# Pacing the first layer's gathers by their own landings instead of by TensorE's marks

## The chip, the cores and the metric

The kernel runs on one core of one Trainium2 chip. The metric is the device time of one execution in microseconds; lower is better. The engines are named as the profile names them: PE is TensorE (PEld its weight loads), DVE is VectorE, ACT is ScalarE, POOL is GpSimd, SP is SyncE. SP, ACT and POOL issue DMAs; POOL alone issues the indirect ones that gather rows by a list of indices.

## The reference

Four graph layers follow each other over 8192 nodes of 32 features and 262144 edges. The edges are sorted by their destination `dst`.

```python
edge_index = jnp.stack([src, dst])
x = _layernorm(x + _L0_gnn_ref(x, L0_gnn_weight, src, dst, edge_type_64), axis=-1)
x = _layernorm(x + _L1_gnn_ref(x, edge_index, edge_weight), axis=-1)
x = _layernorm(x + _L2_gnn_ref(x, edge_index), axis=-1)
x = _layernorm(x + _L3_gnn_ref(x, edge_index, edge_attr_4, edge_attr_32, L3_gnn_W1, ...), axis=-1)
```

The first layer takes for each edge a 32 x 32 matrix by the edge's type, multiplies the source node's row by it and sums the results by destination:

```python
w_e = jnp.take(weight, etypes, axis=0)
h_src = jnp.take(feat, src, axis=0)
msg = jnp.einsum('ei,eio->eo', h_src, w_e)
out = jax.ops.segment_sum(msg, dst, num_segments=N_NODES)
```

The second and third sum source rows by destination, weighted by `edge_weight` and plain. The fourth runs a small network on each edge's 32 attributes and combines its output with the source row.

## The kernel before

**The table and the first layer.** PE multiplies every node's row by all 64 matrices beforehand, and the products are stored in `rel_table` in device memory, 8192 x 64 rows of 32 numbers. The first layer then only gathers one row of this table for each edge and sums by destination. The edges are cut into 128 chunks of 2048: 16 tiles (`TILES`) of 128 edges. One indirect DMA of POOL gathers one tile (128 rows of 128 bytes) into `gathered`, so a chunk is 16 gathers, and the whole first layer 2048. `gather_chunk` issues the 16 gathers of one chunk. It first waits for the chunk's indices (`idx_in[s]`, a load of `key_i` by SP as soon as DVE has released the slot `s`), and each gather raises `rows_in[0][s]` by 16 when it has landed. PE sums the chunk with 16 matmuls against a one-hot matrix (`scatter_chunk`, L1074), which waits for `rows_in`, and DVE adds the sum to `acc` (L1669) and releases the slot.

**The strip rounds.** Beside the first layer the kernel prepares the second and third: it builds for each of 128 strips of destinations a dense matrix of edge weights (`adj`, 2 MB a strip) and one of edge counts (`counts`, 0.5 MB). DVE makes the one-hots (L1637 to L1640), PE multiplies them (L1124, `strip_half`), ACT copies the products out of PSUM (L805, L806) and stores them (`strip_rows`, issues at L808 and L810). Its two staging buffers make ACT wait, before a strip, for the landing of the store of two strips earlier. There are 32 rounds; a round is 4 strips (8 halves, each of 4 groups of 8 matmuls; a matmul of this shape leaves two records in the trace) and, on PE, 3 chunks' scatters, before the halves 0, 3 and 6. So 96 chunks (`EARLY`) are gathered and summed in the rounds, in three slots (`TRIO`). From round 12 on (`AHEAD`) each round also loads two 1 MB pieces of `adj` and multiplies them (L1149).

**The late chunks.** The remaining 32 chunks are summed after the rounds, in four slots, each followed by a set of the second layer's matmuls (L1182).

**POOL's pace.** The semaphore `pe_mark` counts marks. `MARKS_0` names, for each half of a round, the matmuls of `strip_half` that raise it: twelve a round. Before every fourth gather of a round, `marks_0` makes POOL wait for the next mark; `LEAD_0` sets how far POOL is ahead (6 marks, 24 gathers). The wait for the n-th group of four is for mark n - 5 counted in the same way. In the late chunks PE raises two marks a chunk (in the scatter or the set behind it), and POOL waits before every eighth gather, again six marks ahead. The first three chunks are gathered without any pace. The last layer, which gathers from `x_rows` in four slots, already waits every eight gathers for the landing of the gathers before (`RESTS_3`, `rests_3`).

The code here runs if the edges have a regular spread (`is_regular`); another path, untouched, stands behind the test.

## Time and profile before

| | us |
|---|---|
| median of 3 runs | 7251.59 |
| lowest, highest | 7243.55, 7280.37 |
| the profiled execution | 7251.99 |
| its span, first to last instruction | 7250.2 |
| strip rounds, from the second on | 383 to about 3010 |
| late chunks and second layer's matmuls | about 3010 to 3910 |
| third layer | about 3910 to 4220 |
| last layer | 4220 to 7250 |

All the views are of one profiled execution. Times in them are microseconds from the span's start. In the timeline the bracket at the end of a row is how long the engine sat idle before it, and what ended that: another engine's instruction, a DMA's landing, or "issue", which is time in which the engine waited for nothing that the profile shows. "remote" stands for a semaphore's raise for which the profile has no instruction; where records of matmuls are missing, a wait for PE reads so.

### The profile page before, as it was taken

To read this page: it belongs to the slowest core of one execution; us is meant where nothing else is said; L and a number is where in the kernel's file an instruction comes from. 1 tells how busy PE (TensorE), PEld (TensorE's weight loads), DVE (VectorE), ACT (ScalarE), POOL (GpSimd) and SP (SyncE) were. 2 spreads that over 40 slices of the span, in tenths; PEclk is the share of its full clock that TensorE was granted. 3 is DMA by queue.
4 is the path that set the end of the run, shared out by engine and by line. 5 is a ranking of instruction groups with operands and counts; after the bars stand their busy time and mean duration, and the time that the engine had idled before them with its cause. 6 is when DMAs were issued, how large, how long until landed. Compare 5 with 4: busy or idle time off the path is not lost.

```text
span 7250.2 us, 118009 instructions
## 1 busy us (share of the span) xinstructions
PE 5598.4 (77%) x38929; PEld 4300.2 (59%) x38930; DVE 4279.9 (59%) x8297; ACT 2999.4 (41%) x7294; POOL 3945.7 (54%) x4168
## 2 busy tenths in 40 slices
PE   7377777777777777666667668888888888888888
PEld 3177777676776766533333346666666666666666
DVE  4166656655556565311111058877887887888788
ACT  4244444444444444200000045555555555555556
POOL 1445555555555555555550146666666666666665
PEclk7587777777777778666667767777777777777777
DMA  9433333444444444687879601111111111111111
GB/s 318 145 150 145 141 136 130 165 162 149 171 151 163 150 162 163 211 283 269 277 242 296 199 15 25 24 23 24 24 24 23 24 24 23 24 24 24 23 25 24
DMA packets 596643, 865.44 MB, mean 119 GB/s; under 512 B 170833, under 2 KB 418706, under 8 KB 579474
## 3 DMA queue, kind: packets, MB, share of 16 engines
q1 hardware_dynamic: 363858, 385.79, 16.8%
q10 hardware_dynamic: 99520, 406.06, 14.2%
q0 software_dynamic: 133120, 71.57, 5.3%
q8 instruction: 102, 1.67, 0.1%
q14 instruction: 43, 0.35, 0.0%
HBM read 455.19 MB, written 406.85 MB: 119 GB/s over the span
## 4 chain that ended last, share of the span: by engine, by line
PE 37%; issue 24%; POOL 23%; another core or an unknown queue 5%; ACT 5%; DMA 3%; DVE 1%; ACTq 1%; POOLq 0%; SPq 0%; DVEq 0%
POOL gathered L626 23%; PE psum L1124 18%; PE psum L1074 9%; PE psum L1182 6%; ACT arena L806 3%; PE psum L1214 2%; DMA gathered<-x_rows,idx 1%; PE psum L1149 1%; ACT arena L805 1%; DMA arena<-counts 1%; PE psum L1016 1%; ACT table_out L724 1%; DMA arena<-adj 0%; DMA rel_table<-arena 0%
## 5 line engine op out<-in xcount | busy, mean ns | idle before, releaser
L626 POOL DMA_INDIRECT gathered<-rel_table,idx x2048 | 1933.6, 944 | 1676.6 <-issue 587.9
L626 POOL DMA_INDIRECT gathered<-x_rows,idx x2048 | 1949.3, 952 | 1443.3 <-issue 825.4
L1305 PE MATMUL psum<-w,arena 65*128 65x256 f32 x4096 | 1192.7, 443 | 214.2 <-DVE arena L1953 149.7
L805 ACT COPY arena<-psum 128x512 f32<-128x512 f32 x1024 | 603.4, 589 | 1562.0 <-PE psum L1124 1107.8
L1305 PEld LDWEIGHTS psum<-w,arena 65*128 65x128 f32 x4096 | 897.9, 227 | 394.2 <-DVE arena L1953 179.2
L1124 PE MATMUL psum<-arena 64*128 64x128 f32 x8192 | 699.7, 328 | 426.5 <-ACT arena L806 263.3
L1074 PEld LDWEIGHTS psum<-arena 128*128 128x128 f32 x4096 | 875.8, 244 | 220.6 <-issue 198.8
L1074 PE MATMUL psum<-arena 128*128 128x184 f32 x4096 | 953.0, 395 | 4.1 <-ACT arena L789 4.1
L1124 PE MATMUL psum<-table_out 64*128 64x128 f32 x8192 | 741.3, 347 | 242.9 <-ACT arena L806 183.9
L1124 PEld LDWEIGHTS psum<-arena 64*128 64x128 f32 x8192 | 637.9, 233 | 480.1 <-issue 258.3
L1124 PEld LDWEIGHTS psum<-table_out 64*128 64x128 f32 x8192 | 686.8, 253 | 288.1 <-ACT arena L805 181.7
L1953 DVE TENSOR_TENSOR arena<-psum,arena 128x256 f32<-128x256 f32 x1536 | 710.2, 490 | 190.4 <-ACT arena L920 153.6
L1074 PE MATMUL psum<-gathered,arena 128*128 128x32 f32 x4096 | 670.4, 327 | 98.8 <-issue 92.8
L910 ACT ACTIVATE arena<-psum,bias 65x512 f32<-65x512 f32 x512 | 324.9, 678 | 1013.7 <-PE psum L1296 644.4
L1074 PEld LDWEIGHTS psum<-gathered,arena 128*128 128x128 f32 x4096 | 653.6, 250 | 143.5 <-issue 136.1
L1296 PE MATMUL psum<-arena,w 32*65 32x512 f32 x1024 | 544.4, 997 | 172.2 <-ACT arena L910 107.1
L776 ACT ACTIVATE arena<-iota,key_all 128x128 f32<-128x128 f32 x2048 | 623.3, 390 | 0.0
L806 ACT CAST arena<-psum 128x512 fp8e4<-128x512 f32 x1024 | 612.1, 598 | 0.0
L1637 DVE TENSOR_TENSOR table_out<-iota,psum 128x2048 f32<-128x2048 f32 x128 | 292.8, 2288 | 485.7 <-PE psum L1124 244.2
L1637 DVE TENSOR_TENSOR arena<-iota,psum 128x2048 f32<-128x2048 f32 x128 | 292.8, 2287 | 476.3 <-PE psum L1124 288.7
L1182 PE MATMUL psum<-arena,xn 128*32 128x256 f32 x2976 | 395.1, 497 | 212.7 <-issue 195.5
L1669 DVE SCALAR_TENSOR_TENSOR acc<-psum,in_first,acc 128x32 f32 x128 | 32.0, 250 | 853.0 <-remote 428.2
(225 smaller groups left out, 5761.0 us busy)
## 6 DMA issues: line engine op xcount, KB each, us to landing
adj<-arena ACTq DMA_DIRECT2D x128, 2048.0 KB
arena<-adj SPq DMA_DIRECT2D x93, 2048.0 KB
counts<-arena ACTq DMA_DIRECT2D x128, 512.0 KB
arena<-counts SPq DMA_DIRECT2D x64, 1024.0 KB, 11.7
arena<-adj SPq DMA_DIRECT2D x40, 1024.0 KB
rel_table<-table_out ACTq DMA_DIRECT2D x32, 1024.0 KB
rel_table<-arena ACTq DMA_DIRECT2D x32, 1024.0 KB
gathered<-rel_table,idx POOLq DMA_INDIRECT x2048
```

The source lines that it names most:

```text
L626: pool.indirect_dma_start(gathered[:, s, j, :], None, rows[l], bass.IndirectOffsetOnAxis(ap=idx[:, s, j:j + 1], axis=0),).then_inc(group_i ...
L776: a = act.activation(onehot[:, s % 2, j, :], iota1[:, :], ACT.Square, scale=-1.0, bias=key_all[:, bass.ds(c * TILES + j, 1)])
L805: act.copy(w_to, made[:, 1]).then_inc(w_out, 1)
L806: act.copy(c_to, made[:, 0], saturate=False).then_inc(c_out, 1)
L910: act.activation(hidden[:, s % 2, q, :], bank_h[q % 2][0:HID + 1, :], ACT.Relu, bias=bias1[:, :]).then_inc(hidden_ready, 1)
L1074: mm = pe.matmul(bank[:, 0:message.shape[-1]], onehot_of(l, s)[:, j, :], message, start=(j == 0), stop=(j == TILES - 1))
L1124: mm = pe.matmul(psum[:, 2 * r + a, 2 * HIS * i:2 * HIS * (i + 1)], oh_lo[h][rows_of, u, :], oh_both[h][rows_of, u, :, :].rearrange("p k c ...
L1182: mm = pe.matmul(psum[F * g:F * g + F, bank_of(m), 4 * STRIP_D * (m % 2):4 * STRIP_D * (m % 2 + 1)] .rearrange("p (s d) -> p s d", d=STRIP_D),
L1296: pe.matmul(bank_h[q % 2][0:HID + 1, :], w1[F * q:F * q + F, :], edge_T[F * q:F * q + F, :], start=True, stop=True, tile_position=(F * q, ...
L1305: mm = pe.matmul(pair[g % 2][:, WN * q:WN * q + WN], hidden[:, s % 2, q, P * g:P * g + P], w2[:, :], start=True, stop=True)
L1637: dve.tensor_tensor(oh_lo[h], over(P), slot_of(0, P), ALU.is_equal).then_inc(half_ready, 1)
L1953: return dve.tensor_tensor(prod_v[:, :, m], split(w[:, :, Q_END:WN], MUL), over_o(zs[:, tiles, ZC + m:5 * MUL:3], MUL), ALU.mult)
```

## The change

In the rounds POOL no longer waits for PE's marks. Instead `rests_0` makes it wait, before the first and the ninth gather of each chunk, until all gathers issued so far have landed: at the ninth, the eight before it of the same chunk, at the first, the last eight of the chunk before. It waits on `rows_in[0]` of the slot concerned, with a register for each of the six places in a round. PE's twelve marks a round are gone from `strip_half`. The late chunks keep their two marks a chunk. Since the counter now starts with them, the first round of late chunks is written out by itself: chunks 96, 97, 98 (its first six halves) wait for no mark and for no landing, and from chunk 99 on POOL waits for mark 1, 2, 3, as before six marks ahead.

```diff
-MARKS_0 = [{8}, {2, 27}, {20}, {2, 27}, {20}, {13}, {0, 21}, {8, 30}]
+RESTS_0 = (0, 8)
-                by_round = sum(len(marks) for marks in MARKS_0)
-                def marks_0(j):
-
-                    if j % (TRIO * TILES // by_round) == 0:
-                        mark_passed()
+                rounds = {(s, rest): pool.alloc_register(f"round_{s}_{rest}") for s in range(TRIO) for rest in RESTS_0}
+                for s in range(TRIO):
+                    for rest in RESTS_0:
+                        pool.reg_mov(rounds[s, rest], 16 * (TILES * (s > 0 or rest > 0) + (rest or TILES)))
+
+                def rests_0(s):
+
+                    def pace(j):
+
+                        if j in RESTS_0:
+                            pool.wait_ge(rows_in[0][(s - (j == 0)) % TRIO], pool.snap(rounds[s, j]))
+                            pool.reg_add(rounds[s, j], rounds[s, j], 16 * TILES)
+                    return pace
...
-                pool.reg_mov(mark, by_round + 1 - LEAD_0)
...
-                        gather_chunk(0, s, marks_0)
-                pool.reg_mov(mark, ROUNDS * by_round + 1 - LEAD_LATE)
-                with looped(pool, 0, LATE // SLOTS):
+                        gather_chunk(0, s, rests_0(s))
+                def marks_first(s):
+
+                    def pace(j):
+
+                        if j % (TILES // MARKS_LATE) == 0 and s * MARKS_LATE + j * MARKS_LATE // TILES >= LEAD_LATE:
+                            mark_passed()
+                    return pace
+
+                pool.reg_mov(mark, 1)
+                for s in range(SLOTS):
+                    gather_chunk(0, s, marks_first(s))
+                with looped(pool, 1, LATE // SLOTS):
...
-                            if 2 * u + a in marks:
-                                mm.then_inc(pe_mark, 1)
```

On POOL, in the loop of the rounds, before; a row is a wait or a run of gathers, `idx_in_0` the indices of slot 0:

```order
L622 ISA [waits idx_in_0]
L648 REGISTER_ALU [waits pe_mark]
L626 DMA gathered<-rel_table,idx 128x32 x4
L648 REGISTER_ALU [waits pe_mark]
L626 DMA gathered<-rel_table,idx 128x32 x4
L648 REGISTER_ALU [waits pe_mark]
L626 DMA gathered<-rel_table,idx 128x32 x4
L648 REGISTER_ALU [waits pe_mark]
L626 DMA gathered<-rel_table,idx 128x32 x4
```

The same place in the changed kernel, for the first two chunks of a round; `rows_in_first_2` counts what has landed in slot 2 in the first layer:

```order
L622 ISA [waits idx_in_0]
L660 REGISTER_ALU [waits rows_in_first_2]
L626 DMA gathered<-rel_table,idx 128x32 x8
L660 REGISTER_ALU [waits rows_in_first_0]
L626 DMA gathered<-rel_table,idx 128x32 x8
L622 ISA [waits idx_in_1]
L660 REGISTER_ALU [waits rows_in_first_0]
L626 DMA gathered<-rel_table,idx 128x32 x8
L660 REGISTER_ALU [waits rows_in_first_1]
L626 DMA gathered<-rel_table,idx 128x32 x8
```

The four waits of a chunk for PE have become two for POOL's own gathers, each behind eight gathers instead of four.

On POOL, behind the rounds, in the changed kernel; before, each chunk stood here as twice a wait for `pe_mark` and eight gathers:

```order
L622 REGISTER_ALU [waits idx_in_0]
L626 DMA gathered<-rel_table,idx 128x32 x16
L622 REGISTER_ALU [waits idx_in_1]
L626 DMA gathered<-rel_table,idx 128x32 x16
L622 REGISTER_ALU [waits idx_in_2]
L626 DMA gathered<-rel_table,idx 128x32 x16
L622 ISA [waits idx_in_3]
L647 REGISTER_ALU [waits pe_mark]
L626 DMA gathered<-rel_table,idx 128x32 x8
```

The first three late chunks wait for their indices alone; the fourth waits for marks.

On PE, around the first scatter of the first round, before; the rows of the changed kernel are the same but for their line numbers (L1091 and L1141):

```order
L1124 MATMUL psum<-table_out 128x128 [waits c_out,w_out]
L1124 MATMUL psum<-table_out 128x128 x7
L1074 MATMUL psum<-gathered,arena 128x32 [waits added_first,onehot_ready_first,rows_in_first_0]
L1074 MATMUL psum<-gathered,arena 128x32 x15
L1124 MATMUL psum<-arena 128x128 [waits c_out,w_out,half_ready]
```

Nothing moves on PE: the scatter waits for its rows as before, and the strips' matmuls for ACT's copies.

## Rows read from the trace of the kernel before

**Rows 1.** The page: each engine's busy time, share, instructions; the first layer's gathers

```profile
PE 5598.4 (77%) x38929; PEld 4300.2 (59%) x38930; DVE 4279.9 (59%) x8297; ACT 2999.4 (41%) x7294; POOL 3945.7 (54%) x4168
L626 POOL DMA_INDIRECT gathered<-rel_table,idx x2048 | 1933.6, 944 | 1676.6 <-issue 587.9
```

**Rows 2.** Table of stretches: window, length, busy times of engines, granted clock, DMA share

```profile
383.00:1309.00 926.00, 692.92 (x6974) 651.75 (x6973) 557.39 (x532) 382.73 (x728) 517.44 (x548) 0.78 0.37 139
1310.00:2990.00 1680.00, 1279.16 (x12773) 1163.18 (x12774) 1005.71 (x1097) 726.25 (x1335) 905.11 (x959) 0.77 0.46 160
...
4220.00:7250.00 3030.00, 2625.90 (x9763) 1930.27 (x9763) 2443.26 (x6287) 1716.33 (x4986) 1888.97 (x1984) 0.74 0.11 24
```

**Rows 3.** The chain of work, cut to 383 to 2990 us, by line

```profile
by line: PE psum L1124 48.9%; PE psum L1074 18.3%; issue 13.1%; ACT arena L806 7.6%; another core or an unknown queue 5.9%; PE psum L1149 2.1%; ACT arena L805 2.1%; ACTq L810 0.6%; ACTq L808 0.6%; PE psum L1108 0.3%; ACTq L804 0.2%; ACT st 
```

**Rows 4.** Waits of PE, 383 to 3015 us: total, times, longest

```profile
PE psum L1124 <- ACT arena L806: 412.9, 306, 7.0
```

**Rows 5.** PE's scatter L1074, 383 to 2990 us: what ended its waits

```profile
  issue: 77.9, 138
```

**Rows 6.** Timeline of SP: start, length, index loads; idle before in brackets

```profile
1514.79 54.85 SPq L503 DMA_DIRECT2D idx<-key_i  x3
...
1598.08 0.50 SPq L503 DMA_DIRECT2D idx<-key_i  x1
...
2982.89 33.26 SPq L503 DMA_DIRECT2D idx<-key_i  x2
```

**Rows 7.** Timeline of POOL at the start of late chunks 97 and 98

```profile
2985.43 0.94 POOL L626 DMA_INDIRECT gathered<-rel_table,idx  x1 [4.82 <-DMA idx<-key_i]
...
3019.91 0.94 POOL L626 DMA_INDIRECT gathered<-rel_table,idx  x1 [13.28 <-DMA idx<-key_i]
```

**Rows 8.** Timeline of POOL in one round: waits for marks, and a plain pause

```profile
1571.86 0.94 POOL L626 DMA_INDIRECT gathered<-rel_table,idx  x1 [5.64 <-PE psum L1124]
1573.10 0.94 POOL L626 DMA_INDIRECT gathered<-rel_table,idx  x1 [0.30 <-issue]
...
1578.34 0.94 POOL L626 DMA_INDIRECT gathered<-rel_table,idx  x1 [1.80 <-remote]
```

**Rows 9.** Timeline of POOL in the last layer: a wait for landing after eight gathers

```profile
4515.13 0.94 POOL L626 DMA_INDIRECT gathered<-x_rows,idx  x1 [2.03 <-DMA gathered<-x_rows,idx]
```

**Rows 10.** Waits of POOL, whole span: total, times, longest

```profile
POOL gathered L626 <- DMA gathered<-x_rows,idx: 268.2, 127, 3.0
```

**Rows 11.** DMA, 500 to 900 us: queue, packets, MB, share of 16 engines; issues

```profile
q10 hardware_dynamic: 5808, 53.22, 32.7%
q0 software_dynamic: 7680, 3.95, 5.4%
...
adj<-arena ACTq DMA_DIRECT2D x20, 2048.0 KB
```

**Rows 12.** DMA, 1310 to 2990 us: SP's queue, and its loads of adj

```profile
q1 hardware_dynamic: 91200, 42.44, 10.1%
...
arena<-adj SPq DMA_DIRECT2D x40, 1024.0 KB
```

**Rows 13.** Timeline, all engines, near gathers and in a pause of POOL

```profile
1499.15 2.29 DVE L1637 TENSOR_TENSOR arena<-iota,psum 128x2048 f32<-128x2048 f32 x1 [0.16 <-PE psum L1124]
...
1501.00 0.58 ACT L805 COPY arena<-psum 128x512 f32<-128x512 f32 x1 [0.68 <-PE psum L1124]
...
1570.72 0.58 ACT L805 COPY arena<-psum 128x512 f32<-128x512 f32 x1 [5.64 <-PE psum L1124]
```

**Rows 14.** Timeline of PE: third and fourth group of the half h = 6

```profile
1543.78 1.16 PE L1124 MATMUL psum<-table_out 64*128 64x128 f32 x16 [0.37 <-ACT arena L806]
1546.11 1.16 PE L1124 MATMUL psum<-table_out 64*128 64x128 f32 x16 [1.17 <-issue]
```

**Rows 15.** Waits of ACT, 383 to 2990 us: total, times, longest

```profile
ACT arena L805 <- PE psum L1124: 1083.3, 575, 7.9
...
ACT arena L805 <- issue: 68.3, 54, 7.9
```

More of the change, by code:

```diff
@@ L33 @@
 AHEAD = 12
-MARKS_0 = [{8}, {2, 27}, {20}, {2, 27}, {20}, {13}, {0, 21}, {8, 30}]
+RESTS_0 = (0, 8)
 MARKS_LATE = 2
 RESTS_3 = (0, 8)
-LEAD_0, LEAD_LATE = 6, 6
+LEAD_LATE = 6
 AHEAD_HI = 2
@@ L1109, in turn_slots, with strip_half @@
                 t.then_inc(slots_turned, 1)
-            def strip_half(h, due, ready, slots_due=None, marks=()):
+            def strip_half(h, due, ready, slots_due=None):
                 pe.wait_ge(half_ready, ready(2 * h + 2))
@@ L1163, in strip_round @@
                     strip_half(h % 2, lambda n: due(GROUPS * (h // 2) + n), lambda n: ready(4 * (h // 2) + n),
-                               slots_due if h == 2 * SLOTS - 1 else None, MARKS_0[h])
+                               slots_due if h == 2 * SLOTS - 1 else None)
                     if h >= 2 * SLOTS - 2 and ahead is not None:
```

## The prediction

> **What bounds the kernel now.** I read the page first: POOL is busy for 54% of the span, half of that with the first layer's 2048 gathers [rows 1]. A mean over stages says little here, so the next view is the table of stretches [rows 2]. The change touches the strip rounds (383 to 2990 us), and the first 48 gathers behind it. The last layer (4220 to 7250) also gathers on POOL and takes 3030 us, but not one of its instructions moves.
>
> Who sets the time of the strip rounds? The chain of work cut to that stretch is 48.9% PE at L1124 (the strip matmuls), 18.3% PE at L1074 (the scatter of gathered rows), 7.6% and 2.1% ACT at L806 and L805, 13.1% "issue" [rows 3]. POOL is not in it. PE's waits in the stretch say the same: 412.9 us for ACT's cast alone, and no row for a gather [rows 4]. The only PE instruction that needs gathered rows is L1074; what ended its waits is "issue" alone, 77.9 us over 138 times, and no wait of it is put down to a gather [rows 5]. The reader should take from this that POOL has work that nobody waits for. The change can cost time only if POOL becomes late, and it can save time only through something that POOL or the marks do to others.
>
> How early POOL is can be read from the index loads. The loads of slots' indices are issued three within 54.85 us from 1514.79 on, and the next at 1598.08 [rows 6]: three a round, 83.3 us for a round, each as soon as DVE has added the chunk that held the slot. An index load reaches POOL some 2.5 us after its issue (2982.89 to 2985.43, [rows 6, 7]). The slot whose indices are asked for at 1514.8 is scattered a round later, near 1590 us: POOL has about 75 us for 16 gathers that take 16 x 1.245 = 20 us.
>
> **The change, part by part.** First, POOL in the rounds. Before, a round on POOL is 48 gathers of 0.944 us [rows 1], 36 pauses of 0.30 between gathers and 12 waits for marks; a wait for a mark takes 1.8 us at most places and 5.6 at the longest shown [rows 8]. The floor of POOL is so about 45.3 + 10.8 + 12 x 1.8 = 77.7 us a round. After, twelve waits become six, each for the landing of the eight gathers before it: 45.3 + 42 x 0.30 = 57.9 us, and six rests. No rest of this kind stands in the first layer. The nearest rows are the last layer's, which has the same wait every eight gathers: 2.03 us in one [rows 9], 268.2 us over the 127 that are put down to a landing, so 2.1, and 3.0 at the longest [rows 10]. That is the lower bound, since the DMA engines are busy there for 0.11 of the time and in the strip rounds for 0.37 to 0.46 [rows 2]. The upper bound comes from the stores. The queue of ACT's stores takes 32.7% of 400 us in which 20 strips are stored, so 6.5 us for one strip (adj and counts) [rows 11]. A landing that falls behind such a pair waits 3.3 us for its second half on average, so a rest costs at most 2.1 + 3.3 = 5.4 us if every one is caught. Taken: a third is caught, 2.1 + 0.33 x 3.3 = 3.2 us, nearer to the last layer's row because it is the same instruction. From round 12 on the loads of two 1 MB pieces of adj add 10.1% for 40 loads in 1680 us, 4.2 us each [rows 12]: another 0.1 x 2.1 = 0.2, so 3.4. The sum is 57.9 + 6 x 3.2 = 77.1 us for the early rounds and 57.9 + 6 x 3.4 = 78.3 for the late ones. A round now takes 80 us early (five rounds, 20 strips, in the 400 us of [rows 11]) and 83.3 to 84 late (20 rounds in 1680 us [rows 12]). POOL stays under both, by 3 and by 5 us, so it remains the index load that POOL waits for last, and PE and ACT that set the round: **0 us**. What hides the rests is this slack of the rate and, chunk by chunk, the 75 - 28 = 47 us between the end of a chunk's gathers and its scatter.
>
> On that wait a row and a rule stand beside each other. The gathers and the stores are on different queues in the trace, q0 and q10 [rows 11]; no row shows how one stands behind the other. The Trainium skill (DMA: Bandwidth & Descriptors, section on SWDGE, HWDGE and iDMA) says that an engine alternates between its queues; by that rule a landing would not sit out the rest of a store, a rest would cost near 2.1 us and POOL's round 70.5. The forecast is the same; the slower rival below would be less likely than I make it.
>
> Second, when gathers run. Without marks POOL starts a chunk as soon as its indices are in. They lead by more than before and then stop, where now fours are spread over the round. The bytes are the same: q0 takes 5.4% of the engines' time [rows 11]. Nobody waits for an earlier gather, so no gain. Do gathers slow others while they are issued? Beside two gathers, at 1499.80 and 1501.05, a one-hot of DVE took 2.29 us and a copy of ACT 0.58 [rows 13]; the copy is no longer than the one of 0.58 at 1570.72, while POOL paused before its gather of 1571.86 [rows 8, 13]. I take **0 us**.
>
> Third, PE loses twelve increments a round, 384 in all. They ride on matmuls that stay. The seventh half of a round (h = 6) has marks on its matmuls 0 and 21, so its third group of 16 records holds a mark and its fourth none: both take 1.16 us [rows 14]. A bound from above is the time of one matmul, two of these records, 1.16/8 = 0.145 us, 384 times: 56 us of gain. From below nothing. Taken: **0**, since the two read equal.
>
> Fourth, the 48 gathers of chunks 96 to 98, which lose their marks and get no rests. Chunks 97 and 98 already wait for their indices and not for marks: 4.82 and 13.28 us [rows 7]. Only chunk 96 can start earlier, and the wait of 13.28 us for chunk 98 behind it swallows that. Chunk 99 on keeps its marks: the register starts at 1 on an empty counter, where it stood at 385 on a counter at 384, so the same matmul releases it. **0 us.** Behind POOL's new waits nothing else is queued than its own gathers; SP and ACT, which issue the loads and stores, are not moved.
>
> The sum is 0 against the profiled run's own time, 7251.99 us (span 7250.2), which stands 0.4 us above the median of the three runs; these reach from 7243.6 to 7280.4. About 0.5%, 36 us, is what a measurement of this kernel can tell from no change.
>
> **Rivals.** (A) POOL becomes the bound of the strip rounds. If the landing stands behind a store at most rests, POOL's round is 57.9 + 6 x 5.4 = 90.3 us: 10.3 above 80 for the 11 looped early rounds and 6.6 above 83.7 for the 20 late ones, 113 + 132 = +245 us, **7497**. It decides from a rest of (80 - 57.9)/6 = 3.7 us in the early rounds and 4.3 in the late ones; at 4.3 throughout only the early ones stretch, by 3.7 x 11 = 41 us, 7293. For it: the distance to 3.7 is half a microsecond, and my 3.2 is an estimate. Against it: POOL starts each stretch well ahead, and the longest rest of the last layer is 3.0.
>
> (B) Stores land earlier. ACT may not begin a strip before the store from two strips earlier has landed; of its waits in this stretch 68.3 us before L805 are put down to nothing ("issue", 54 times) [rows 15]. If these were such stores, slowed by gathers, and the new order clears them, the round is shorter by 68 us in all: **7184**. With it goes the case of the increments, 56 us, 7196. Against both: 1083.3 us of ACT's waits name PE's matmuls, and the bytes are unchanged.
>
> (C) The change does not do what it says, because the index load is always last and the rests are over when it arrives. Within a chunk, at its ninth gather, this can't be so, since the eight before were just issued; at its first it may. The time is that of the forecast.
>
> **How the numbers follow.** No change within 0.5%, 7215 to 7288: 0.69 (my sum 0.63, C 0.06). A 0.11, with its half towards 7293 and the rest beyond. Other small losses of this kind 0.03. B and the increments, each beyond 36 us, 0.17 together. The likeliest is my sum, 7251. The range of 8 in 10 takes in B's 7184 and A's near end of 7293: 7184 to 7305; A's far end is left out. Faster 0.17, same 0.69, slower 0.14.
>
> **What would show it.** In the profile after, a round of strips should take 80 and 84 us again (three index loads apart); POOL's waits should name landings of gathers, some 190 of about 2 to 5 us, 3.3 on average, and loads of indices, which appear once in this stretch now; none should name PE before 3000 us; PE's L1074 should again wait for no gather. The prediction is wrong if L1074 waits for gathers or POOL enters the chain before 2990 us (A), if ACT's "issue" waits fall while the stage shortens (B), or if the granted clock of the stage leaves 0.77 to 0.78 [rows 2] with the same idle times.

## The result and the profile after

| | before | changed |
|---|---|---|
| median of 4 runs, us | 7247.57 | 7829.04 |
| lowest, highest | 7242.22, 7280.37 | 7814.12, 7855.48 |
| ratio of changed to before | | 1.080, 95% interval 1.076 to 1.084 |
| span of the profiled execution | 7250.2 | 7812.7 |
| mean of 31 strip rounds | 83.7 | 102.2 |

The change costs 581 us; the forecast was none. A round is measured here from one of DVE's additions of slot 2 to `acc` (L1669, now L1684) to the next. 31 rounds longer by 18.5 us make 573 us. The stages behind the rounds take what they took: from the rounds' end to the last layer's first addition (the late chunks, the second layer's matmuls and the third layer) 1245 us (1269 before), from there to the end 2968 (2965). L1124 is now L1141, L1074 is L1091, ACT's copy and cast are L822 and L823, DVE's one-hot is L1652.

The page of the changed kernel, engines and gathers, as in [rows 1]:

```profile
PE 5785.3 (74%) x38929; PEld 4507.6 (58%) x38930; DVE 4279.2 (55%) x8297; ACT 3007.3 (38%) x7294; POOL 3941.5 (50%) x4168
L626 POOL DMA_INDIRECT gathered<-rel_table,idx x2048 | 1932.6, 944 | 2243.2 <-DMA idx<-key_i 1118.8
```

DVE's and ACT's instructions did not get longer: their busy times are those of before, and a gather takes 944 ns again. PE's busy time is 187 us more with the same number of instructions. The stretches show why, in the columns of [rows 2]:

```profile
400.00:1500.00 1100.00, 759.29 (x6794) 717.15 (x6794) 544.05 (x523) 375.26 (x711) 501.09 (x531) 0.67 0.31 115
1500.00:3580.00 2080.00, 1407.75 (x12917) 1295.30 (x12918) 1007.80 (x1100) 737.91 (x1346) 908.85 (x964) 0.69 0.37 129
4840.00:7812.00 2972.00, 2559.24 (x9584) 1899.51 (x9584) 2409.88 (x6202) 1683.70 (x4893) 1874.19 (x1972) 0.75 0.11 24
```

The granted clock of the rounds is 0.67 to 0.69, where it was 0.78 and 0.77: a lower share of the time goes at the higher of its two levels. The last layer stands at 0.75 (0.74 before). Over the 31 rounds PE is busy for 2151 us where it was 1958, with as many matmuls (19.6 thousand records): some 6 us of the 18.5 a round are its own instructions at the lower clock. The other 12 are idle time of PE, and on DVE and ACT nearly all of the new time is idle. The waits of ACT, POOL and PE from 400 to 3600 us (total, times, longest) name it:

```profile
ACT arena L822 <- PE psum L1141: 1049.5, 543, 9.9
ACT arena L822 <- remote: 963.2, 234, 12.2
ACT arena L822 <- issue: 25.7, 29, 3.9
```

```profile
POOL gathered L626 <- DMA idx<-key_i: 1002.0, 83, 22.5
POOL gathered L626 <- issue: 500.6, 1354, 2.2
POOL gathered L626 <- DMA gathered<-rel_table,idx: 271.1, 69, 6.6
```

```profile
PE psum L1141 <- ACT arena L823: 578.6, 257, 13.9
```

Three things stand in them. POOL does not bound the rounds: 83 times it waits for indices, 12.1 us on average, and only 69 of its 186 rests end on a landing by this view (271.1/69 = 3.9 us each). PE waits for no gather (L1091 has "issue" waits alone, 171.5 us); it waits for ACT's cast, 579 us where it was 413 [rows 4]. (Another 279 us before L1141 read "issue", 148 before; nearly all of them are waits for ACT's copy and cast too.) And ACT's row that names "remote" is 963 us in 234 waits. In the trace of before the row reads so (not shown ahead of the prediction; it stands between the two of [rows 15]):

```profile
ACT arena L805 <- remote: 304.7, 112, 10.0
```

That is 659 us more on "remote" and 34 us less on PE's matmuls (1083.3 in [rows 15]). In the chain of waits the share "another core or an unknown queue", the chain's name for the same thing, goes from 5.9% [rows 3] to 21.1%. There is no other core here.

What is such a wait? A stretch of the changed kernel's timeline, all engines (rows between left out):

```profile
2009.15 0.94 POOL L626 DMA_INDIRECT gathered<-rel_table,idx  x1 [12.11 <-DMA idx<-key_i]
...
2011.65 2.22 PE L1141 MATMUL psum<-arena 64*128 64x128 f32 x32
...
2013.91 2.29 DVE L1652 TENSOR_TENSOR table_out<-iota,psum 128x2048 f32<-128x2048 f32 x1 [6.49 <-remote]
...
2017.88 0.94 POOL L626 DMA_INDIRECT gathered<-rel_table,idx  x1 [0.30 <-issue]
2020.49 0.59 ACT L822 COPY arena<-psum 128x512 f32<-128x512 f32 x1 [8.98 <-remote]
2020.95 0.94 POOL L626 DMA_INDIRECT gathered<-rel_table,idx  x1 [2.13 <-DMA gathered<-rel_table,idx]
...
2021.71 0.59 PE L1141 MATMUL psum<-arena 64*128 64x128 f32 x2 [7.84 <-ACT arena L823]
```

POOL issues eight gathers back to back, from 2009.15 to 2018.82. PE ends two groups of the strip at 2013.87. ACT stands idle with nothing left to do but the copy of their product; it starts at 2020.49, 6.6 us after PE's end and 1.7 after the end of the eighth gather. PE then needs ACT's copies and has idled 7.84 us itself. No record is missing: PE's 32 pieces are there, and in both traces all 16384 records of the strips' matmuls are. What comes late is the raise of the semaphore by PE's last matmul, and because it comes so long after the matmul's end, the profile does not connect the two and writes "remote". The trace also keeps the times at which this semaphore rose: of the 295 copies in the changed kernel that start more than 2 us after their matmul's end, with ACT idle before them, 291 start within 0.06 us of such a rise (209 of 214 before). The profile models the ends of matmuls, so a late end could look the same; but in 209 of the 295 cases PE began 16 or more further records before the copy started. The same stands in the profile of before, on a run of four gathers (timeline, all engines), and it could have been read there:

```profile
1552.50 1.16 PE L1124 MATMUL psum<-arena 64*128 64x128 f32 x16 [0.59 <-ACT arena L806]
...
1555.46 0.94 POOL L626 DMA_INDIRECT gathered<-rel_table,idx  x1 [0.30 <-issue]
1556.33 0.58 ACT L805 COPY arena<-psum 128x512 f32<-128x512 f32 x1 [3.97 <-remote]
```

The matmuls end at 1553.66, the copy starts at 1556.33, 2.7 us later.

To count this, each group's last matmul was paired with ACT's copy of that group (960 groups of the rounds). This "lag" holds ACT's other work too, but at an undisturbed handover, with ACT idle, it is 0.04 us. Its mean goes from 1.50 to 2.18 us, and the sum over lags above 2 us from 1064 to 1984. Sorted by POOL's state (a run ends where POOL pauses for more than 1.2 us): of 668 groups that end while POOL is in a run of gathers, 223 are copied within 0.3 us, 187 later but within the run, and 258 after the run, at a time that scatters little: 1.8 us after the end of its last gather (median; eight in ten between 1.5 and 2.7), 1.1 in the kernel before. Which of them are prompt depends on how far the run has come. With ACT idle before the copy, 109 of the 113 groups that end beside the first gather of a run are copied within 0.3 us, 39 of 102 beside the second, and 1 of 175 from the fourth on; outside runs it is 222 of 223. In the kernel before it is 92 of 119 beside the first and 6 of 108 from the fourth on. The other direction, ACT to PE, is prompt in and out of runs: 0.14 us.

This is **theory H**, the hold: while POOL issues indirect gathers back to back, many of PE's raises reach the engines that wait for them late, most of these only when the run is over. Runs of eight hold longer than runs of four, which the marks made. The rivals at this point were that the rests themselves are the price (a landing, not a hold), that the marks on PE's matmuls did something useful by being there, that the gathers now stand at a worse place of the round, that POOL being busy is enough, that any small DMA does it, and that the scattered rows do it.

### The profile page after: what moved, and what is told of

It reads as the page before. It is cut to its first block, busy times and chain, and to the rows that moved or that the text cites. A ratio compares the mean times of both kernels' runs of the same rounds, so it can differ in the third digit from the quotient of the medians.

```text
span 7812.7 us, 117630 instructions
## 1 busy us (share of the span) xinstructions
PE 5785.3 (74%) x38929; PEld 4507.6 (58%) x38930; DVE 4279.2 (55%) x8297; ACT 3007.3 (38%) x7294; POOL 3941.5 (50%) x4168
## 4 chain that ended last, share of the span: by engine, by line
PE 34%; issue 25%; POOL 21%; another core or an unknown queue 11%; ACT 4%; DMA 3%; DVE 1%; ACTq 1%; SPq 0%; POOLq 0%; DVEq 0%
POOL gathered L626 21%; PE psum L1141 16%; PE psum L1091 9%; PE psum L1197 5%; ACT arena L823 3%; PE psum L1229 1%; DMA gathered<-x_rows,idx 1%; DMA arena<-counts 1%; PE psum L1033 1%; ACT arena L822 1%; ACT table_out L741 0%; PE psum L1164 0%; DMA arena<-adj 0%; DMA rel_table<-arena 0%
## 5 line engine op out<-in xcount | busy, mean ns | idle before, releaser
L822 ACT COPY arena<-psum 128x512 f32<-128x512 f32 x1024 | 603.1, 589 | 2133.4 <-PE psum L1141 1062.8
L1141 PE MATMUL psum<-table_out 64*128 64x128 f32 x8192 | 830.1, 377 | 472.1 <-ACT arena L823 298.3
L1141 PE MATMUL psum<-arena 64*128 64x128 f32 x8192 | 763.6, 347 | 543.2 <-ACT arena L823 320.7
L1141 PEld LDWEIGHTS psum<-table_out 64*128 64x128 f32 x8192 | 772.5, 282 | 517.3 <-ACT arena L822 289.5
L1141 PEld LDWEIGHTS psum<-arena 64*128 64x128 f32 x8192 | 695.2, 252 | 598.7 <-ACT arena L822 299.9
L1091 PEld LDWEIGHTS psum<-arena 128*128 128x128 f32 x4096 | 888.6, 247 | 223.2 <-issue 198.7
L1091 PE MATMUL psum<-arena 128*128 128x184 f32 x4096 | 963.4, 398 | 5.6 <-ACT arena L806 5.6
L1091 PE MATMUL psum<-gathered,arena 128*128 128x32 f32 x4096 | 741.0, 346 | 106.6 <-issue 100.3
L1091 PEld LDWEIGHTS psum<-gathered,arena 128*128 128x128 f32 x4096 | 720.5, 272 | 151.6 <-issue 148.2
L1652 DVE TENSOR_TENSOR arena<-iota,psum 128x2048 f32<-128x2048 f32 x128 | 292.7, 2287 | 844.9 <-remote 415.4
L1652 DVE TENSOR_TENSOR table_out<-iota,psum 128x2048 f32<-128x2048 f32 x128 | 292.7, 2287 | 659.0 <-PE psum L1141 389.2
L823 ACT CAST arena<-psum 128x512 fp8e4<-128x512 f32 x1024 | 609.4, 595 | 0.0
L1684 DVE SCALAR_TENSOR_TENSOR acc<-psum,in_first,acc 128x32 f32 x128 | 32.0, 250 | 880.8 <-remote 385.9
```

Of the source, the lines that this page charges most:

```text
L822: act.copy(w_to, made[:, 1]).then_inc(w_out, 1)
L823: act.copy(c_to, made[:, 0], saturate=False).then_inc(c_out, 1)
L1091: mm = pe.matmul(bank[:, 0:message.shape[-1]], onehot_of(l, s)[:, j, :], message, start=(j == 0), stop=(j == TILES - 1))
L1141: mm = pe.matmul(psum[:, 2 * r + a, 2 * HIS * i:2 * HIS * (i + 1)], oh_lo[h][rows_of, u, :], oh_both[h][rows_of, u, :, :].rearrange("p k c ...
L1652: dve.tensor_tensor(oh_lo[h], over(P), slot_of(0, P), ALU.is_equal).then_inc(half_ready, 1)
```

## The experiments

Ratios are to the kernel before on the same chip; where a kernel has one timing, its time stands beside the median of before there. Round and lag are the means described above. Chips differ, so a chip's number stands with each; which chip the result is from is not known.

| kernel | chip | us | before there | ratio | round | lag |
|---|---|---|---|---|---|---|
| before | | 7247.6 | | 1 | 83.7 | 1.50 |
| changed | | 7829.0 | 7247.6 | 1.080 | 102.2 | 2.18 |
| e1_rest4 | 0 | 7744.0 | 7416.9 | 1.043 | 95.7 | 1.17 |
| e2_idle_marks | 0 | 7950.8 | 7416.9 | 1.072 | 103.5 | 2.19 |
| e3_marks8 | 0 | 8099.9 | 7416.9 | 1.092 | 108.1 | 2.38 |
| e4_memset | 0 | 6535.4 | 7416.9 | 0.881 | 58.1 | 0.12 |
| e5_busy, e6_plain, e7_sp | 3 | 6051 to 6056 | 6152.2 | | 57 | 0.1 |
| e8_marks16 | 3 | 6154.8 | 6152.2 | 1.0005 | 59.9 | 0.13 |
| e9_after_again | 6 | 7826.1 | 7260.6 | 1.079 | 102.0 | 2.14 |
| e10_busy | 6 | 6451.6 | 7260.6 | | 58.2 | 0.13 |
| e11_plain | 6 | 6433.5 | 7260.6 | | 58.0 | 0.11 |
| e12_sp | 6 | 6445.6 | 7260.6 | | 57.8 | 0.18 |
| e13_near | 13 | 7837.6 | 7238.2 | | 102.3 | 2.14 |
| e14_free | 13 | 8175.3 | 7238.2 | 1.129 | 113.2 | 2.97 |
| e15_marks16 | 13 | 7458.5 | 7238.2 | 1.030 | 90.4 | 1.69 |

### How long a run is

**e1_rest4**, the changed kernel with a rest every four gathers:

```diff
-RESTS_0 = (0, 8)
+RESTS_0 = (0, 4, 8, 12)
```

> The changed kernel with a rest every four gathers instead of every eight (twelve waits for a landing a round). Theory H (hold): while POOL issues gathers back to back, what PE completes reaches ACT and DVE only when POOL pauses, so a run of eight gathers (10 us) holds PE's completions up to 10 us and a run of four (5 us) at most 5. Then the wait of ACT behind PE falls back to the kernel before's, and what is left is POOL's own rate, 45.3 + 36 x 0.30 + 12 x 2.1 to 2.6 = 81 to 87 us a round: 7250 to 7400 us. Theory M (the increments of the marks on PE kept its completions moving): no recovery, 7830. Theory P (place: gathers now start right behind the release of a slot, at a bad place of the round, however long a run is): no or little recovery, 7700 to 7830.

Measured 1.043 (1.039 to 1.047), round 95.7. ACT's lag falls to 1.17, below that of before. But now POOL is the bound; its waits and PE's from 400 to 3380 us:

```profile
POOL gathered L626 <- DMA gathered<-rel_table,idx: 1215.3, 370, 6.7
...
PE psum L1091 <- DMA gathered<-rel_table,idx: 438.4, 66, 16.1
```

That is 3.3 us a rest, and no wait for indices any more. 45.3 + 36 x 0.30 + 12 x 3.3 = 95.7 us, the measured round; the 81 to 87 us that were expected had a rest at 2.1 to 2.6 us. Twice as many rests make the kernel faster than the changed one (1.072 on this chip with idle marks, e2 below), which the theory that the rests are the price excludes, and what is left is POOL's own rate.

**e3_marks8**, the kernel before with six marks a round instead of twelve, so that PE's marks pace POOL in runs of eight, with no landing anywhere:

```diff
-MARKS_0 = [{8}, {2, 27}, {20}, {2, 27}, {20}, {13}, {0, 21}, {8, 30}]
+MARKS_0 = [{8}, {27}, set(), {2}, {20}, set(), {0}, {8}]
...
-LEAD_0, LEAD_LATE = 6, 6
+LEAD_0, LEAD_LATE = 3, 6
```

> The kernel before with six marks a round instead of twelve (every second one of them kept), three marks ahead: POOL waits for PE as before, but before every eighth gather. No landing is waited for. Theory H: runs of eight gathers hold PE as in the changed kernel, 7600 to 7850. Theory M: half of the increments are left, 7250 to 7540. Theory P: the gathers stay spread over the round, 7250 to 7350.

Measured 1.092 (1.089 to 1.096), round 108.1, lag 2.38. The slowdown is there without one landing wait: it is the length of the run, whatever ends it. It is even larger than in the changed kernel. The gathers stay spread over the round here, so their place is not the cause either.

**e2_idle_marks**, the changed kernel with the twelve raises a round put back on PE's matmuls, which nobody in the rounds waits for:

```diff
+MARKS_0 = [{8}, {2, 27}, {20}, {2, 27}, {20}, {13}, {0, 21}, {8, 30}]
...
-                pool.reg_mov(mark, 1)
+                pool.reg_mov(mark, ROUNDS * sum(len(marks) for marks in MARKS_0) + 1)
...
+                            if 2 * u + a in marks:
+                                mm.then_inc(pe_mark, 1)
```

> The changed kernel with PE's twelve marks a round put back on its matmuls, while POOL does not wait for them in the rounds (it starts waiting at mark 385, in the late chunks). Theory M: back to 7250. Theories H and P: 7830, as changed.

Measured 1.072 (1.068 to 1.077), round 103.5. The raises neither cost nor help to within what two chips differ; that PE made them was not what the change lost.

**e14_free**, no pace at all in the rounds, so runs of sixteen:

```diff
-                        gather_chunk(0, s, rests_0(s))
+                        gather_chunk(0, s)
```

> The changed kernel without its rests: sixteen gathers of a chunk run without a pause, held back by the index load alone. Theory H, by the length of a run: the hold reaches up to 20 us, ACT more than 2.2 us late on average, rounds of 105 to 115 us, ratio to before 1.09 to 1.15. If the rests' own waits made the loss: rounds back towards 84 us, ratio about 1.00. If the length does not matter beyond eight: as changed, 1.08.

Measured 1.129 (1.122 to 1.136), round 113.2, lag 2.97, the slowest of all, though nothing but its indices makes POOL wait. Its timeline, all engines, in one run of sixteen and behind it:

```profile
1504.73 0.38 PE L1141 MATMUL psum<-arena 64*128 64x128 f32 x3
...
1509.83 0.58 ACT L822 COPY arena<-psum 128x512 f32<-128x512 f32 x1 [6.02 <-remote]
...
1511.05 2.08 PE L1141 MATMUL psum<-arena 64*128 64x128 f32 x16 [5.93 <-ACT arena L822]
...
1520.03 0.94 POOL L626 DMA_INDIRECT gathered<-rel_table,idx  x1 [0.31 <-issue]
1522.52 0.58 ACT L822 COPY arena<-psum 128x512 f32<-128x512 f32 x1 [11.62 <-remote]
```

The last matmul ends at 1513.13, its copy starts at 1522.52, 9.4 us on. The raise before, of 1505.11, came 4.7 us late but within the run. With runs of 4, 8 and 16 a raise that is held past the run arrives 1.1, 1.8 and 3.0 us (medians) after the last gather of the run ended. That it grows with the run, and that raises beside a run's first gather are prompt, would fit a backlog that the gathers build up and that drains behind them; no run looked into it.

**e8_marks16 and e15_marks16** are one kernel on two chips, the kernel before with sixteen marks a round, so a wait before every third gather:

```diff
-MARKS_0 = [{8}, {2, 27}, {20}, {2, 27}, {20}, {13}, {0, 21}, {8, 30}]
+MARKS_0 = [{2, 18}] * 8
...
-LEAD_0, LEAD_LATE = 6, 6
+LEAD_0, LEAD_LATE = 8, 6
...
-                    if j % (TRIO * TILES // by_round) == 0:
-                        mark_passed()
+                        if (s * TILES + j) % (TRIO * TILES // by_round) == 0:
+                            mark_passed()
```

> The kernel before with sixteen marks a round, evenly two in each half (matmuls 2 and 18), so that POOL waits before every third gather, eight marks ahead. Theory H: runs of three hold PE less than runs of four, and a wait for a mark costs POOL 1.8 us; POOL's own floor is 45.3 + 32 x 0.30 + 16 x 1.8 = 83.7 us a round, that of the kernel before was 77.7 with rounds of 81 to 84. So no gain: 0 to 3% slower than before (7420 on this chip), 7420 to 7640, POOL the bound. If the hold weighs more than POOL's rate: 7250 to 7400.

> The kernel of e8 (before, with sixteen marks a round and runs of three gathers), which ran on a chip without the hold at a ratio of 1.0005. On a chip with it: by the length of a run ACT is less late than before's 1.5 us, 1.0 to 1.3; but POOL's floor of 83.7 us a round becomes the bound, rounds of 84 to 90 us, ratio 1.00 to 1.03. If the hold weighs more than POOL's rate, below 1.00.

e8 fell on a chip without the hold (below) and says nothing of it. e15 was to be less late than the kernel before (1.0 to 1.3 us) and bound by POOL; it came out at 1.030 (1.025 to 1.035), round 90.4, with a lag of 1.69 and no wait of PE for a gather. The ratio lies in what was expected, the reason does not. A mark makes a pause only if PE has not passed it, and many had been passed: of 496 waits 278 paused for more than 1.2 us, and 203 of the runs were of six gathers, 54 of three. The kernel before has 279 runs of four of its 326. With runs of mostly six the lag lies between that of four and of eight; a version with real runs of three was not made.

### Is it the gathers?

The next kernels leave the first layer's gathers of rounds 1 to 31 out and put something else in their place; the sums of the first layer are therefore not those of the reference, and the strips, which are what is timed here, are computed in full.

**e4_memset**, a memset of the tile of rows (POOL, about 0.1 us) for each gather; the rests and PE's scatters wait for the memsets' count instead of the gathers':

```diff
...
+                    if stand_in:
+                        pool.memset(gathered[:, s, j, :], 1.0).then_inc(stand[s], 16)
+                        continue
...
-                        gather_chunk(0, s, rests_0(s))
+                        gather_chunk(0, s, rests_0(s), True)
```

> The changed kernel without the 1488 gathers of the rounds 1 to 31: POOL writes each tile with a memset of 128x32 instead, so the sums of the first layer are not the reference's; waits and order are otherwise the same. Theory H: nothing holds PE, ACT starts within 0.1 us of PE's end throughout, and the rounds get shorter than those of the kernel before too (which has runs of four): 65 to 75 us a round, 6700 to 7000 us in all. Theory M: 7830, since the marks are still gone. Theory P: 7250 at best, as before.

Measured 0.881 (0.878 to 0.885), and a round of 58.1 us, less than the 65 to 75 that were expected. In the profile of before a round takes 83.7; by the times on this chip alone the difference is (7416.9 - 6535.4)/31 = 28 us a round. So the gathers, which the profile shows on no critical path, cost the kernel *before* 25 to 28 us of every round. Not all of it is waiting: PE is busy for 1601 us in these 31 rounds where it was 1958, since the clock is higher. ACT's waits from 300 to 2213 us:

```profile
ACT arena L828 <- PE psum L1147: 671.5, 572, 14.0
ACT arena L828 <- remote: 65.4, 5, 37.4
```

The "remote" waits are gone but for five, and the lag is 0.12 us. The granted clock of the stage stands at 0.89 (0.77 before).

Three kernels then asked what of a gather does it. **e5_busy** keeps POOL busy (an iota of 128 x 256 and the memset for each gather), **e6_plain** lets POOL issue a plain DMA of the same size from consecutive rows of `rel_table`, **e7_sp** lets SP issue those, with POOL idle:

```diff
...
+                        pool.iota(gathered[:, TRIO, 0:8, :].rearrange("p a b -> p (a b)").bitcast(I32), [[1, 8 * F]], base=1, channel_multiplier=0).then_inc(extra["onehot"], 1)
+                        pool.memset(gathered[:, s, j, :], 1.0).then_inc(stand[s], 16)
```

```diff
...
+                        pool.dma_start(gathered[:, s, j, :], rel_table[P * (TILES * s + j):P * (TILES * s + j) + P, :]).then_inc(rows_in[l][s], 16)
```

```diff
...
+                        sp.dma_start(gathered[:, s, j, :], rel_table[P * (TILES * s + j):P * (TILES * s + j) + P, :]
+                                     ).then_inc(stand[s], 16)
```

> As e4, the changed kernel without the 1488 gathers of rounds 1 to 31, but POOL is kept busy: before each memset stands an iota over 128x256 numbers into an unused slot, so that POOL works about 1 us for each tile as it does with a gather. The first layer's sums are not the reference's. What holds PE's completions? Theory B (any busy POOL): rounds near 100 us again and ACT late behind PE, 7700 to 8000 us on this chip. Theory D (the indirect DMA: its issue on POOL or its landing): as e4, 58 us a round, 6500 to 6600.

> The changed kernel with the 1488 gathers of rounds 1 to 31 replaced by plain DMAs of POOL, 128 rows of 128 bytes from consecutive places of the table, same waits and same semaphores; the sums of the first layer are not the reference's. Theory D1 (what holds PE is any DMA that POOL issues, or its landing): rounds of 95 to 105 us if POOL's issue takes as long as a gather's. Theory D2 (the indirection: reading indices, scattered rows): 58 to 65 us a round, about 6550.

> The changed kernel with the same 1488 plain DMAs issued by SP behind the chunk's index load, POOL idle in the rounds; the first layer's sums are not the reference's. The same number of landings, each raising a semaphore. Theory D3 (landings, the DMA engines' writes, hold PE): ACT again 2 to 7 us late behind PE and rounds of 80 us or more. Theory D4 (it is POOL's issuing): ACT within 0.1 us behind PE, rounds 58 to 65 us, about 6550.

All three came out at 6051 to 6056 us. But the kernel before took 6152.17 us there (6144.90 to 6157.82, 13 runs), against medians of 7238 to 7417 on the others, and e8, with gathers back to back all through the rounds, shows a lag of 0.13 us. In e8's timeline, all engines:

```profile
1004.40 2.91 PE L1127 MATMUL psum<-table_out 64*128 64x128 f32 x32 [1.99 <-ACT arena L809]
...
1004.81 0.96 POOL L626 DMA_INDIRECT gathered<-rel_table,idx  x1 [0.30 <-issue]
1005.60 0.58 ACT L808 COPY arena<-psum 128x512 f32<-128x512 f32 x1 [0.37 <-PE psum L1127]
1006.07 0.94 POOL L626 DMA_INDIRECT gathered<-rel_table,idx  x1 [0.30 <-issue]
```

The gather takes the same 0.94 us, and ACT's copy starts 0.8 us into one, within POOL's run. This chip does not have the hold (its late chunks are shorter too, 645 us where the other traces have 816 to 871), so the three kernels told nothing apart here. The same three files were run again as e10_busy, e11_plain and e12_sp, beside the changed kernel itself, e9_after_again:

> The changed kernel itself, beside the kernel before, on whichever chip this is. The runs so far fall in two kinds of chip: on one the kernel before took 7242 to 7433 us, with ACT 1.5 us late behind PE on average, on the other 6145 to 6158, with no lateness in rounds of 57 to 60 us. On a chip that shows the hold: ratio 1.07 to 1.09. On a chip that does not: POOL's own rate, 57.9 + 6 x 2.5 to 3.4 = 73 to 78 us, is above the 57 to 60 us that PE and ACT need there, so POOL bounds the rounds: 31 x 14 to 18 = +430 to +560 us, 6600 to 6700, ratio 1.07 to 1.09 too. If POOL's rate does not matter on such a chip: 6150, ratio 1.00.

> The kernel of e5 again (no gathers in rounds 1 to 31, POOL busy with an iota and a memset for each tile), which ran on a chip without the hold. On a chip with it: theory B (any busy POOL holds PE's completions) gives rounds near 100 us and ACT 2 us late on average; theory D (DMAs hold) 58 us and 0.1 us, as e4.

> The kernel of e6 again (plain DMAs of POOL in place of the gathers). On a chip with the hold: if any DMA that POOL issues holds PE, ACT is late by 2 us on average and the rounds take 80 to 105 us; if only the indirect ones do, 0.1 us and 57 to 60 us, as on the chip of e6.

> The kernel of e7 again (the same plain DMAs issued by SP, POOL idle in the rounds). On a chip with the hold: if the landings hold PE, ACT is late by 1 us or more and the rounds take 70 us or more; if it is POOL's issuing, 0.1 us and 57 to 60 us.

On chip 6 the changed kernel costs 1.079 (1.075 to 1.082) with a lag of 2.14, as in the result, so the hold is there. And beside it the three take 6433 to 6452 us (one timing each), with rounds of 58 us. In e11 POOL issues, and rests, as in the changed kernel; its groups of instructions and its timeline (all engines):

```profile
L627 POOL DMA_DIRECT2D gathered<-rel_table x1488 | 784.1, 535 | 1004.5 <-DMA gathered<-rel_table 522.5 <-DMA idx<-key_i 447.1 <-issue 34.9
```

```profile
999.51 3.69 POOL L627 DMA_DIRECT2D gathered<-rel_table  x7
1000.83 2.06 PE L1144 MATMUL psum<-table_out 64*128 64x128 f32 x32
1002.04 0.58 ACT L825 COPY arena<-psum 128x512 f32<-128x512 f32 x1 [3.71 <-PE psum L1144]
```

The copy starts inside POOL's run of seven DMAs. So neither a busy POOL, nor plain DMAs of this size from POOL's queue with rests for their landing, nor the same traffic from SP holds PE's raises (lags of 0.11 to 0.18 us). One of POOL's plain DMAs is shorter, 535 ns, so its runs of eight last some 4.2 us and not 9.7; but the share of lags above 2 us is 2 of 960, where the kernel before has 302 with runs of four that last 4.7 us. For e10 the same reserve is larger: its iota takes 342 ns, so POOL is busy for half as long as with a gather, and longer work on POOL was not tried.

**e13_near**, the changed kernel with indices that lie close together (the edges' sorted destinations in place of the keys into `rel_table`), still indirect; it leaves out only that the right rows are gathered:

```diff
+                if near:
+                    sp.dma_start(idx[:, s, :], edge_cols(dst)[:, bass.ds(c, 1), :].rearrange("p c j -> p (c j)")
+                                 ).then_inc(idx_in[s], 16)
+                    return
```

> The changed kernel, but in rounds 1 to 31 the indices are the edges' destinations in place of the rows of the table, so that a gather's 128 rows lie within some 64 neighbouring rows; the same indirect DMAs, waits and bytes. The sums of the first layer are not the reference's. Theory I (the indirect issue holds PE): as changed, rounds of 100 us, ACT 2 us late behind PE. Theory S (reads scattered over the 67 MB table hold PE): rounds of 58 to 75 us and ACT less than 0.5 us late.

Measured 7837.6 us on chip 13, round 102.3, lag 2.14: that of the changed kernel. Where the rows lie does not matter. What is left is POOL's indirect DMA as such; whether it is the indirection or the 944 ns that each keeps POOL was not separated further.

## Why the prediction was wrong, point by point

**The step that failed** is the second part's question: "Do gathers slow others while they are issued?", answered with **0 us**. It was answered from how long a one-hot of DVE and a copy of ACT take beside gathers [rows 13]. That was right and is so still (0.58 us, 2.29 us, and DVE's 4279 us over the kernel). But an engine can be slowed between its instructions too, at the handover from PE, and that was not looked at. It costs 18.5 us a round more than before, and 25 to 28 of before's round (e4), PE's lower clock included.

**The reading behind it.** "remote" was taken, in the explanation of the views, for missing records of matmuls. The 304.7 us of ACT's waits of that kind and the 5.9% of the chain [rows 3] were passed over, and the two together were what grew to 963.2 and 21.1%. A missing record would have left a hole in PE's row; at 1552.50 there is none, nor anywhere in the strips' 16384 records.

**"POOL has work that nobody waits for."** The sentence is right by the waits, and the conclusion, that the change "can save time only through something that POOL or the marks do to others" and cost it only if POOL is late, is where the sign was lost: what POOL does to others can also get worse.

**POOL's rate before.** The floor of 77.7 us was made with 1.8 us for a wait for a mark, from the row of 1578.34 [rows 8]. In the 31 rounds the 326 pauses above 1.2 us take 2.50 on average, 26.3 us a round, and with 45.3 for the gathers and some 11.3 of short pauses POOL's round is 83. That does not make POOL the bound: the pauses are waits for PE's marks, which would fill a round of any length, and PE waits for no gather [rows 4, 5]. The floor was too low by how long the marks really hold POOL, but the slack of 5 us after the change was read rightly: with rests of 3.2 us on average (below) POOL would need 57.9 + 6 x 3.2 = 77 us, and in the changed kernel it waits for indices instead, 1002 us in all. The slack was there; it was the round that grew.

**The rests** were sized well: 3.2 to 3.4 us was taken; 3.3 us is the mean of e1's 370, and in the changed kernel the pause before the ninth gather of a chunk is 3.2 on average over all 93 (3.9 is the mean of the 69 that are put down to a landing; the short ones, 2.2 us, read "issue"). By the rule cited from the Trainium skill (DMA: Bandwidth & Descriptors, section on SWDGE, HWDGE and iDMA), that an engine alternates between queues, a rest was to cost near 2.1; the traces do not agree, by some 1.2 us. Why a landing takes longer in the rounds was not taken apart.

**Rival A**, POOL as the bound, was the rival on the slow side. It did not happen in the changed kernel (no gather in PE's waits, POOL at rest for indices), but 12 rests a round make it real: e1. **Rival B**: ACT's "issue" waits fell from 68.3 to 25.7 us, but the stage grew. **Rival C** came true for the first gather of a chunk, where the index load was last in 82 of 93 cases, and not for the ninth; as it said, that cost nothing. **The increments** at 0: e2 agrees. **The late chunks** at 0: the stages up to the last layer take 1245 us against 1269. **POOL's waits after** were to name indices and some 190 landings of 3.3 us; they name 83 index loads, 12.1 us each, and 69 landings. That POOL is not late came true, without being worth anything.

Of the signs named, the one that came is "if the granted clock of the stage leaves 0.77 to 0.78". The clause "with the same idle times" did not hold: the idle times grew too. Over the runs the two go together (0.89 in rounds of 58 us, 0.77 in 83.7, 0.69 in 102.2, 0.67 in 113.2).

**The hold is shown** by runs: on one chip the lag is 1.17 with runs of four (e1) and 2.19 to 2.38 with eight (e2, e3, by a landing or by marks), on another 1.69 with mostly six, 2.14 with eight and 2.97 with sixteen (e15, e13, e14), and e4 and e10 to e12 take it away with the gathers alone. Run length is not all of it: before, with runs of four too, has 1.50. **Not shown** is what in the chip does it, and why PE's raises and not ACT's. One rival is open: the recording. Every timing here comes with a granted clock, so from an execution that was recorded, and under gathers the trace itself loses records of raises (718 of 1025 of ACT's copies have one in before, 1021 in e4, 1006 on chip 3). Whether an unrecorded execution has the hold, no run says. The hold is not complete either: a third of the raises inside runs are prompt, most of them near the run's start, and in the row of 2013.91 DVE is let go inside a run, 2.2 us after PE's transposes. Nor is it known what differs on chip 3; the changed kernel was not timed there, and the cost of 8% is that of the chips with the hold. It could cost there in another way: POOL would need 57.9 + 6 x 3.3 = 77.7 us a round, an estimate from e1's rests, where e8 shows a round of 59.9.

## What to carry to other kernels

An engine that nobody waits for can still set the time: look not only at how long others' instructions take beside it, but at the time from the end of one engine's instruction to the start of the one that it releases, with and without the suspect running. A wait that the profile puts down to "remote" in a program of one core is a question, not a gap in the records: look up whether the producer's instruction is there and when it ended. Before replacing a wait that looks like overhead, ask what rhythm it imposes; here the marks kept runs of indirect gathers at four, and longer runs made the kernel slower (1.03 with mostly six, 1.07 to 1.09 with eight, 1.13 with sixteen), while leaving the gathers out would be worth 11 to 12%.

## What the runs showed of the hardware that was not expected

- On three of four chips, and on that of the result, while POOL issues indirect DMAs of 128 rows back to back (0.944 us each, 0.30 apart), raises of semaphores by PE arrive late: on average over all groups 1.2 to 1.5 us with runs of 4, 2.1 to 2.4 with 8, 3.0 with 16 (0.12 without gathers). Those held past the end of a run come 1.1, 1.8 and 3.0 us behind it. Beside the first gather of a run they are prompt (109 of 113 in the changed kernel), from the fourth on they are not (1 of 175).
- Plain DMAs of the same bytes, from POOL (535 ns each) or SP, and POOL busy with an iota do not do this (0.11 to 0.18 us).
- One chip of four runs the kernel before in 6152 us where the other three take 7238 to 7417 (medians), with a lag of 0.13 us under gathers back to back.
- A landing of a run of gathers takes 3.3 us after the last issue in the rounds, where the DMA engines are busy for 0.37 of the time, and 2.1 us in the last layer at 0.11 [rows 10].
